# Seven of eight expert batches moved into the gated linear attention, which becomes one block

## The reference

```python
# layer 1, experts (x: 8 x 512 x 128, c_fc: 8 x 128 x 512, c_proj: 8 x 512 x 128)
h = jnp.einsum('ecd,edf->ecf', buf, c_fc)
h = jnp.square(jax.nn.relu(h))
expert_out = jnp.einsum('ecf,efd->ecd', h, c_proj)
out = jnp.sum(gathered * probs_masked[..., None], axis=1)
# layer 2, gated linear attention: 8 heads of 32, complex
u = jax.nn.silu(x @ W_in.T + b_in)
q, k, v, a = complex parts of (u @ W_qkva.T + b_qkva)
a = a * (rsqrt(|a|^2) * sigmoid(log(|a|^2)))
h[t] = a[t] * h[t-1] + k[t] v[t]^T           # 32 x 32 complex state per head, h[-1] = h0
y = q h ; y2 = silu(y @ W_y.T + b_y) ; return y2 @ W_out.T + b_out
```

## Time and profile before

| what | value |
|---|---|
| median of 3 launches | 4452.96 us (4449.75 to 4459.58) |
| the profiled launch | 4450.96 us |
| its span in the trace | 4449.0 us |
| PE, DVE, ACT, POOL busy | 85%, 53%, 34%, 17% |
| experts | 767.4 to 1213 us |
| gated linear attention | 1229 to 2513 us |
| mean granted TensorE clock | 0.808 of full speed |

### The profile page before, as it was taken

The page is one execution under the profiler, slowest core; times in us unless marked ns, Lnnn a source line. Parts: engine busy times, 40 slices in busy tenths (PEclk is TensorE's granted clock), DMA queues, the critical chain, the costliest instruction groups (busy, mean ns, idle before and its releaser), DMA issues. The chain is left out here.

```text
span 4449.0 us, 124857 instructions
## 1 busy us (share of the span) xinstructions
PE 3796.8 (85%) x55640; PEld 2398.6 (54%) x55640; DVE 2365.0 (53%) x6027; ACT 1509.0 (34%) x2783; POOL 736.4 (17%) x724
## 2 busy tenths in 40 slices
PE   4877775999948887878787795999999999999986
PEld 2336662444325555556565442566666666666672
DVE  3757773332268777777777111244444444444445
ACT  2643332555432222222222142333333333333323
POOL 1212221000011112121211000222222222222210
PEclk9886666999955556555655697999999999999967
DMA  2000001322000000000000001000000000000000
GB/s 80 0 1 1 1 1 30 47 38 38 17 1 3 3 3 3 3 3 3 3 3 3 16 1 58 1 2 2 2 2 2 2 2 2 2 2 2 2 2 21
DMA packets 18968, 45.93 MB, mean 10 GB/s; under 512 B 4864, under 2 KB 8321, under 8 KB 17409
## 3 DMA queue, kind: packets, MB, share of 16 engines
q1 hardware_dynamic: 18432, 37.95, 3.6%
HBM read 35.71 MB, written 2.23 MB: 9 GB/s over the span
## 5 line engine op out<-in xcount | busy, mean ns | idle before, releaser
L2008 PE MATMUL ps<-d_hp,d_w_qk 128*128 128x512 f32 x1024 | 546.3, 629 | 2.7 <-DVE d_hp L2265 2.7
L1227 PE MATMUL ps<-g_Q,g_K 32*32 32x32 f32 (+1 forms) x12288 | 272.7, 249 | 21.9 <-issue 7.5
L1227 PEld LDWEIGHTS ps<-g_Q,g_K 32*32 32x32 f32 x12288 | 238.3, 136 | 65.0 <-PE ps L1227 39.0
L2086 POOL TENSOR_TENSOR d_sq<-d_QK 128x512 f32<-128x512 f32 x128 | 133.0, 1039 | 763.6 <-ACT d_QK L2128 761.0
L1048 PE MATMUL ps<-ex_hs,w_c_fc 128*128 128x512 f32 x512 | 232.6, 598 | 19.4 <-DVE ex_hs L1014 19.4
L1022 DVE TENSOR_TENSOR ex_r<-ex_r 128x512 f32<-128x512 f32 x128 | 88.4, 692 | 277.1 <-ACT ex_r L1036 277.1
L1036 ACT ACTIVATE ex_r<-ps 128x512 f32<-128x512 f32 x256 | 151.5, 592 | 235.5 <-PE ps L1048 235.5
L1259 PE MATMUL ps<-g_S,g_V 32*64 32x32 f32 x4096 | 161.5, 288 | 81.8 <-DVE g_H L1435 63.4
L1059 PE MATMUL ps<-ex_r,w_c_proj 128*128 128x512 f32 x512 | 230.0, 592 | 0.0
L2008 PEld LDWEIGHTS ps<-d_hp,d_w_qk 128*128 128x128 f32 x1024 | 162.7, 191 | 82.2 <-issue 63.4
L2106 ACT ACTIVATE d_F<-ps 128x128 f32<-128x128 f32 x256 | 70.9, 277 | 379.5 <-PE ps L1922 378.4
(11 more groups left out here) (467 smaller groups left out, 8040.8 us busy)
## 6 DMA issues: line engine op xcount, KB each, us to landing
ex_root<-gate_rows SPq DMA_DIRECT2D x8, 2048.0 KB, 15.1
d_QK<-in_conv_qk_dram SPq DMA_DIRECT2D x2, 2048.0 KB, 8.2
X<-in_x_dram SPq DMA_DIRECT2D x1, 2048.0 KB, 10.8
w_c_fc<-in_c_fc_dram SPq DMA_DIRECT2D x1, 2048.0 KB, 8.0
w_c_proj<-in_c_proj_dram SPq DMA_DIRECT2D x1, 2048.0 KB, 12.4
out_dram<-X SPq DMA_DIRECT2D x1, 2048.0 KB, 6.3
w_wmod<-in_wmod_dram SPq DMA_DIRECT2D x1, 1536.0 KB, 6.4
w_w<-in_w_dram SPq DMA_DIRECT2D x2, 768.0 KB, 5.0
```

Of the source, the lines that this page charges most:

```text
L1227: ins = e.matmul(later(scored, n_), keys_, queries(n_, planes, r, 4 * i + j), start=(turn_ == 0 and part == 0 and n_ != 1), stop=(part == ...
L2008: ins = e.matmul(b, w_qk[:, j, c, ts(H, C)], hp_of(u)[:, j:j + T], start=(j == 0), stop=(j == TAPS - 1))
L2086: e.tensor_tensor(squares(x), qk, qk, ALU.mult).then_inc(pool.steps, pool.did(f"{tag}sq{x}"))
```

## The change

- `experts` is called with `batches = 1`. It does batch 0 only, and also stores its input (all 8 batches, 2 MB) to a new DRAM tensor `h_rows`.
- `gla` does batches 1 to 7 of the experts, half a batch (four experts) in each of its first 14 stages (`eb`, `half`). For each expert `SyncE` fetches the broadcast root, the 256 KB of `c_fc` and the 256 KB of `c_proj` from DRAM into rings of two slots, with four new semaphores. DVE scales the input (`root`), PE does 16 `up` and 16 `down` products in a stage (12 `down` in a half 0, 20 in a half 1, since `down` runs four behind), ACT does Relu and Square of every one, and DVE adds the sum to X (`residual`).
- The scores and gains of all pieces now use one pair of banks, P[0] and P[1]; P[2] holds the `up` product and P[3] the `down` sum. So `scores(i + 1)` waits for `sums(i)` and `states(i)`.
- `scores` and `outputs` are cut into quarters that stand alternately in the list, with an `up` or a `down` between some of them. `project` is cut into `decay`, `query` and `key`. `sums(3)` and `states(3)` stand ahead of `turned`.
- The 19 blocks become one. The semaphore clears and table loads between them go; in their place each step waits by name for the steps of the stage before that it depends on.

```diff
-        ORDER = (("copy", 0), ("keys", 0), ("scores", 0), ("turn", "decays"), ("turn", "values"), ("gains", 0), ("scores", 1), ("make", "center"),
...
-                 ("outputs", 2), ("make", "units"), ("turn", "turned"), ("sums", 3), ("states", 3), ("out", "hidden"), ("outputs", 3),
-                 ("out", "gate"), ("turn", "split"), ("out", "gated"), ("out", "last"))
+        ORDER = (("copy", 0), ("keys", 0), ("scores", (0, 0)), ("turn", "decays"), ("scores", (0, 1)), ("scores", (0, 2)), ("scores", (0, 3)), ("gains", 0),
+                 ("make", "center"), ("root", 0), ("up", 0), ("down", -4), ("sums", 0), ("states", 0), ("make", "spread"), ("up", 1), ("down", -3),
+                 ("up", 2), ("down", -2), ("make", "normed"),
+
+                 ("scores", (1, 0)), ("outputs", (0, 0)), ("up", 3), ("turn", "run0"), ("scores", (1, 1)), ("outputs", (0, 1)), ("down", -1),
+                 ("scores", (1, 2)), ("outputs", (0, 2)), ("scores", (1, 3)), ("outputs", (0, 3)), ("outputs", (0, 4)), ("turn", "values"), ("gains", 1),
+                 ("root", 1), ("up", 4), ("down", 0), ("sums", 1), ("states", 1), ("make", "hidden"), ("up", 5), ("down", 1), ("make", "gate"),
+
+                 ("scores", (2, 0)), ("outputs", (1, 0)), ("up", 6), ("turn", "run1"), ("scores", (2, 1)), ("outputs", (1, 1)), ("down", 2),
+                 ("scores", (2, 2)), ("outputs", (1, 2)), ("make", "gated"), ("scores", (2, 3)), ("outputs", (1, 3)), ("outputs", (1, 4)), ("gains", 2),
+                 ("root", 2), ("up", 7), ("down", 3), ("sums", 2), ("states", 2), ("make", "decay"), ("up", 8), ("down", 4), ("turn", "blocks"),
+
+                 ("scores", (3, 0)), ("outputs", (2, 0)), ("make", "query"), ("scores", (3, 1)), ("outputs", (2, 1)), ("scores", (3, 2)),
+                 ("outputs", (2, 2)), ("make", "key"), ("scores", (3, 3)), ("outputs", (2, 3)), ("outputs", (2, 4)), ("gains", 3), ("turn", "carry"),
+                 ("up", 9), ("down", 5), ("make", "units"), ("sums", 3), ("states", 3), ("root", 3), ("up", 10), ("down", 6), ("turn", "turned"),
+
+                 ("outputs", (3, 0)), ("up", 11), ("outputs", (3, 1)), ("outputs", (3, 2)), ("down", 7), ("outputs", (3, 3)), ("outputs", (3, 4)),
+                 ("out", "hidden"), ("make", "logs"), ("up", 12), ("down", 8), ("out", "gate"), ("up", 13), ("down", 9), ("turn", "split"), ("up", 14),
+                 ("down", 10), ("up", 15), ("down", 11), ("out", "gated"), ("out", "last"), ("down", 12), ("down", 13), ("down", 14), ("down", 15),
+                 ("residual", 0))
...
+        stage(None, None, None, 0, 0, None, 1, 0)
+        stage(None, None, 0, 0, 1, None, 1, 1)
+        for b in range(B):
+            more, extra = b + 1 < B, b + 2 < B
+            stage(1 if b else None, 0, 1, b + 1 if more else None, 0 if more else None, b - 1 if b else None, b + 2 if extra else None, 0 if extra else None)
+            stage(0, 1, 0 if more else None, b + 1 if more else None, 1 if more else None, None, b + 2 if extra else None, 1 if extra else None)
+        stage(1, None, None, None, None, B - 1, None, None)
...
+                    def up(i):
+                        n, f = i // 4, i % 4
+                        if f == 0:
+                            e.wait_ge(dve.steps, dve.at(now(f"hs{n}")))
+                            e.wait_ge(up_slot[n % 2].steps, up_slot[n % 2].at(now(n)))
+                        if i:
+                            e.wait_ge(act.steps, act.at(now(f"r{i - 1}")))
...
+                        e.matmul(P[2], fc[:, n % 2, ts(f, C)], hs[:, n % 2], start=True, stop=True).then_inc(pe.steps, pe.did(now(f"u{i}")))
...
+                        e.matmul(P[3], proj[:, n % 2, f, :], r[:, (16 * c["half"] + i) % 5], start=(c["half"] == 0 and i == 0),
+                                 stop=(c["half"] == 1 and i == 15)).then_inc(pe.steps, pe.did(now(f"d{i}")))
...
-                    experts(k, k1, gate_rows)
+                    experts(k, k1, gate_rows, h_rows, 1)
```

More of the change, by code:

```diff
@@ L981, in route, with experts @@
         k.end()
-def experts(k, h1, gate_rows):
+def experts(k, h1, gate_rows, h_rows, batches):
     nc = k.nc
     E, F = 8, 4
-    N = B * E
+    N = batches * E
     with ExitStack() as s:
@@ L998, in _ @@
             def _(e):
-                for b in range(B):
+                for b in range(batches):
                     if b >= 2:
@@ L1004, in _ @@
                     e.wait_ge(dma.steps, dma.at(f"root{b}"))
+                e.dma_start(h_rows, h1[:]).then_inc(dma.steps, dma.did("h"))
+                e.wait_ge(dma.steps, dma.at("h"))
             @block.vector
@@ L1099, with gla @@
 LOG_MIN = -19.0
-def gla(k):
+def gla(k, a, gate_rows, h_rows):
     nc = k.nc
@@ new lines, in gla, with stage @@
+        MLP = ("root", "up", "down", "residual")
+        PAIR = {"decay": (0, 1), "query": (2, 3), "key": (4, 5)}
+        PRODUCTS = [(j, ri) for j in (2, 0, 1) for ri in range(2)]
+        STAGES = []
+        def stage(copy_g, sg, tg, mb, mg, ob, eb, half):
+            STAGES.append({"n": len(STAGES), "copy_g": copy_g, "sg": sg, "tg": tg, "mb": mb, "mg": mg, "ob": ob, "eb": eb, "half": half})
+        stage(None, None, None, 0, 0, None, 1, 0)
+        stage(None, None, 0, 0, 1, None, 1, 1)
@@ new lines, in make @@
+                            if c["tg"] is not None:
+                                e.wait_ge(dve.steps, dve.at(now("v0")))
+                            e.matmul(P[6], k.w["W_in2"][:], h[:], start=True, stop=True).then_inc(pe.steps, pe.did(now("z")))
+                        elif what in PAIR:
+                            if what == "decay" and c["mg"] == 0:
+                                e.wait_ge(dve.steps, dve.at(now("u")))
+                            if what == "decay" and c["tg"] is not None:
+                                e.wait_ge(dve.steps, dve.at(now("v1")))
+                            for x in PAIR[what]:
+                                j, ri = PRODUCTS[x]
@@ L1315, in out @@
                         elif what == "last":
-                            e.wait_ge(dve.steps, dve.at("gated"))
-                            e.matmul(P[7], k.w["W_out2"][:], h2[:], start=True, stop=True).then_inc(pe.steps, pe.did("out"))
-                    in_turn(keys=keys, scores=scores, gains=gains, outputs=outputs, turn=turn, make=make, out=out)
+                            e.wait_ge(dve.steps, dve.at(now("gated")))
+                            e.matmul(P[7], k.w["W_out2"][:], h2[:], start=True, stop=True).then_inc(pe.steps, pe.did(now("out")))
@@ L1321, in _ @@
+                    in_turn(keys=keys, scores=scores, gains=gains, outputs=outputs, turn=turn, make=make, out=out, up=up, down=down)
                 @block.scalar
@@ L1567, in _, with root @@
-                    in_turn(sums=sums, states=states, make=make, turn=turn, out=out)
-            k.end()
+                            e.wait_ge(act.steps, act.at(now("out")))
+                            x = flat(k.X[:, c["ob"]:c["ob"] + 1, :])
+                            e.scalar_tensor_tensor(x, o2[:], m(c["ob"], 2, GA), x, ALU.mult, ALU.add).then_inc(dve.steps, dve.did(now("last")))
+                    def root(n):
+                        if n == 0 and c["half"] == 0:
+                            e.wait_ge(dma.steps, dma.at(now("hx")))
+                        e.wait_ge(up_slot[n % 2].steps, up_slot[n % 2].at(now(n)))
+                        e.tensor_tensor(hs[:, n % 2], hx[:], hs[:, n % 2], ALU.mult).then_inc(dve.steps, dve.did(now(f"hs{n}")))
@@ new lines, in residual @@
+                    def residual(_):
+                        if c["half"]:
+                            e.wait_ge(pe.steps, pe.at(now("d15")))
+                            x = flat(k.X[:, c["eb"]:c["eb"] + 1, :])
+                            e.scalar_tensor_tensor(x, P[3], m(c["eb"], 1, GB), x, ALU.mult, ALU.add).then_inc(dve.steps, dve.did(now("residual")))
+                    in_turn(sums=sums, states=states, make=make, turn=turn, out=out, root=root, residual=residual)
+            k.end(k.slots)
```

540 lines of the change are left out of this document (297 added, 243 removed).

## The result

The changed kernel takes 4289.0 us (4279.9 to 4298.5), the kernel before 4453.9 us beside it: a ratio of 0.963, 95% interval 0.961 to 0.9645. Forecast were 4242 us with a range from 4110 to 4420. The profiled execution took 4287.2 us, its span is 4285.4 us, 163.6 us less than before. The forecast sum was -211 us.

A forecast was written before the change was run, and what follows sets the result against it. The prediction took PE to bound the kernel, running at a mean clock of 0.58 in the scan stages. Its terms, -385 + 165 + 16 - 7 = -211 us, gave a median of 4242 us, range 4110 to 4420.

The forecast's parts named there:

- step 2: The 12 scan stages that get dense expert work: 89.6 us each, 1075 us in all, +165 us.
- step 4: The last five stages, which get no dense work: four terms together -7 us (-35 to +30).
- Step 1: Experts' stage: seven of the eight batches leave it, 55.0 us each, -385 us.
- step 3: The two preparing stages, which get 55 us of dense work: +16 us (0 to 40).
- Rivals B: 12 dense stages: the mix does not raise the clock above 0.58, stage 115 us, kernel 4568 us; chance 0.11.
- C: 12 dense stages: the mix holds the upper clock nearly throughout, -156 us, kernel 4086 us; chance 0.14.
- 13 us for the clock: Each of the 12 dense stages: time lost to slow starts and stretches at the lower clock, 13 us.
- Rival D: 12 dense stages: PE and DVE wait for each other, 20 us a stage, kernel 4420 us; chance 0.15.
- block starts: Last five stages: five block starts go, -21 us.
- the single bank pair: Last five stages: DVE's hand-over lies bare, 3 us for three pieces of four stages, +36 us.
- `outputs(3)`: Last five stages: its wait for the last states gets shorter, -7 us.
- drains: Last five stages: waits between score quarters are covered by the mixing, -15 us at the lower clock.

The follow-up runs named there:

- relu_first: Changed kernel with the output gate and the split moved behind the last `up` and its `down`, so the Relus no longer queue behind them: 4259.3 us, ratio 0.957.
- one_block_alone: Changed kernel's single block and new order, but all 8 expert batches back in the experts' own stage: 4508.0 us, ratio 1.013 to the kernel before.
- states_late: Changed kernel with `sums(3)` and `states(3)` put back behind `turned` in all stages: 4358.5 us, ratio 0.9795.
- late_two_banks_last: two_banks_last with `sums(3)` and `states(3)` moved behind `turned` in the last five stages: 4306.5 us, those stages 319.3 us.
- old_order_last: Changed kernel, still one block, with the order and bank pairs of the kernel before in the last five stages: 4264.5 us, those stages 279.2 us.
- gains_first_last: two_banks_last with each group's outputs behind the next group's gains, not mixed into its scores, in the last five stages: 4287.0 us, those stages 302.1 us.
- downs_quarter: Changed kernel with 128 instead of 512 columns in most `down` products of the attention's stages, leaving out part of the result: 4269.7 us, ratio 0.959.
- two_banks_last: Changed kernel with two pairs of banks and an order of their own in the last five stages: 4279.6 us, those stages 299.4 us.

## Why the prediction was right, and where not

**Right in sign, near in size, right in the main mechanism.** The profiled launch gained 164 us of the 211 forecast; 17 of the missing 47 us are step 2's and 26 are step 4's. Step 1 (-385, was -383), step 3 (+16, was +19, a guess within 0 to 40 that no run took apart) and the stage of step 2 (89.6 us, was 91.0) carry the sum. Rivals B (clock stays at 0.58, stage 115 us) and C (upper clock throughout, 13 us less a stage) are out by the window's 0.86; the four-point table shows that it is the dense work that does it. The experts' weights cost nothing, as forecast: no wait on a transfer is among PE's in the 12 stages.

**Step 2, inside the stage.** The forecast had 84.6 us of PE's work with 13 us for the clock, and 5 of waits; measured were 81.9 busy and 9.1 idle. The two misses nearly cancel, so that the stage came out within 1.4 us is in part luck: PE's work and the clock together were put 2.7 us too dear, the waits 4.1 too cheap. Of the 9.1, 5.1 are the Relus (60.9/12); relu_first takes 4.4 of them away and gets 2.2 back as waits for DVE. The prediction saw the right queue, ACT in order behind DVE, but walked it past the output gate alone, at one Relu in every second stage. It never walked the split's negations (L1496), which stand in ACT's list two places on and cost 4.2 to 6.7 us at once in the stages without output work. A step that is inserted between others has to be checked against all that is queued ahead of it, not the first.

**Rival D** (engines take turns, 20 us of waits) did not come, since dense products cover DVE's hand-over; one_block_alone shows the same lists without that cover, 19.2 us idle a stage. D would have been right for this order without this work.

**Two rows were misread.** The 4.3 us of a block start are 68.2/16, but 37.1 of the 68.2 are one wait, the longest in the same row. It ended at 1311.28 us, at the start of the first scan stage, after a preparing stage in which PE had run out of work. The other 15 are 2.1 us each, and the last five stages of the kernel before have four of them:

```profile
PE ps L1209 <- PEq L70: 8.3, 4, 2.6
```

And the clock did not fall "once" in the bulk of the delta rule. In windows of 20 us from 2830 to 4230 us it is below 1.00 in ten, at lowest 0.83 between 3470 and 3490 us, together some 28 us at the lower level. The mean of 0.99 and what was argued from it stand.

**Step 4 failed: -7 forecast, +19 measured.** Its four terms, by what the runs showed:
- block starts, -21: too large by the misreading, as PE's waits there are 8.3 us. The old order in one block took 279.2 us against 291.9, so -11 to -13 for all that leaving the blocks brought;
- the single bank pair, +36: giving it back, with the order that goes with it, brought 10 to 12 us. I priced a bare DVE hand-over at 3 us, twelve times, and did not ask whether PE had to be on time there; it then waited at the stage's end instead;
- `outputs(3)`, -7: undone in two forms it cost 10 us (states_late, all stages) and 20 us (late_two_banks_last). Larger than forecast, within the new order. In the order of before it costs less: there PE has the whole of scores 3, gains 3 and outputs 2 to do beside `turned`; in the last five stages of the kernel before its trace has 8.7 us of that wait in all, in old_order_last 10.7;
- drains, -15: hidden, as the quarters' rows show (in the changed kernel a quarter of scores and one of outputs take 1.64 us together at 1.2 GHz, 6.6 for four, where the earlier trace rows have 4.75 + 2.87), and worth nothing: gains_first_last gives them back and stays within 3 us.

The last of these says what was wrong in the step as a whole. It summed PE's savings in stages in which PE idles 77 us of 311 and DVE's chain (fourth states, blocks, `turned`, split, gate) sets the end. What counts there is when that chain starts and what PE has left to do beside it. The prediction's own sign for it, longer last stages, came true, though the bank pair it named is 10 to 12 us of the 30 to 32 between this order and the old one. How the rest divides between the place of the key products, the split and others stays open.

**The clock's rule.** The delta rule's tail in the kernel before is at 0.60 with PE busy 87%, the last five stages of old_order_last at 0.59 with 85% (236.26 of 279.20), and the 12 stages of downs_quarter at 0.79 with 87%. In relu_first the 12 stages are at 0.84 with PE busy 93%, in the changed kernel at 0.86 with 90%. The Trainium skill ("TensorE: Matmul & The Clock Gate", section "The HAM clock gate") says that the clock is set by how busy PE has been; read as busy share of the profile, these rows speak against it, and the prediction did well to go by what PE worked on in each row.

## What to carry to other kernels

Dense products cost less than half their time beside small-tile work that runs at the lower clock, since they pay part of it back twice: they fill waits and raise the clock (27.5 us for 11.4 us here against the same order without them, 15.2 us against the old order). They do that only where they are; a stretch that shares the new order but gets no dense work must be costed by itself, and may want its old order. When work is threaded through an in-order queue, walk every instruction that stands ahead of each inserted one on its own engine, and put those that only depend on the fast side (here the Relus) ahead of those that wait for the slow one.

## What was not expected of the hardware

VectorE's and GpSimd's products slow each other. Moving `states(3)` ahead of `turned` took away what lay between VectorE's and GpSimd's halves of the split. Rows of groups (count, busy us, mean ns), from the first stage of 1311 us on in the kernel before, from 947 us on in the changed one:

```profile
L1545 DVE TENSOR_TENSOR g_Q<-g_unit_qh,g_F 128x256 f32<-128x256 f32 (+1 forms) x90 | 44.1, 556 | 0.0
L1199 POOL TENSOR_TENSOR g_K<-g_kh,g_E 128x256 f32<-128x256 f32 (+1 forms) x90 | 79.5, 915 | 107.2 <-DVE g_kh L1537 107.2
...
L1665 DVE TENSOR_TENSOR g_Q<-g_unit_qh,g_F 128x256 f32<-128x256 f32 (+1 forms) x90 | 91.1, 1076 | 0.0
L1245 POOL TENSOR_TENSOR g_K<-g_kh,g_E 128x256 f32<-128x256 f32 (+1 forms) x90 | 104.8, 1195 | 89.9 <-DVE g_kh L1657 89.9
```

The same 90 instructions of VectorE take 556 ns before and 1076 ns after, GpSimd's 915 and 1195. In states_late they are part of the way back, at 806 and 1083. In the last five stages one edit, `sums(3)` and `states(3)` between the two halves or not, moves VectorE's from 943 ns in two_banks_last to 535 in late_two_banks_last, and the pair of timelines above has 6.88 us and 3.16 us for the same six. The Trainium skill ("GPSIMD Engine Reference", section "Specifications") says that the two share their SBUF interfaces and contend when a VectorE instruction has two SBUF inputs; the rows agree and give the price, nearly a factor of two. It lies on the path in the last five stages and in the dense ones too: in the stage with the 4.24 us wait above, VectorE's six products take 6.89 us from 1477.73 us on beside GpSimd's 7.11 us from 1477.23 us on, and the negations in front of the Relu wait for just these. How much of the kernel's time it costs was not measured apart.
